# A fused attention and LoRA expert kernel: the last exponential first, router and masks behind the value products, masks read from PSUM, row and gate work of the next batch moved forward

## What is computed

```python
h = _layernorm(x) * (1 + ca) + sa
x = x + ga * attn(h)          # attn: norm, q k v, causal softmax(q k / 16) v, o_proj, + h
h = _layernorm(x) * (1 + cb) + sb
# feed-forward of h:
base_out = silu(gate_base) * up_base @ Wd.T
probs = softmax(xf @ Wr.T); topw, topi = top_k(probs, 2)
# for each chosen expert e, with weight w_e:
hh = silu(gate_base + g_lora_e) * (up_base + u_lora_e)
acc += w_e * (hh @ Ad_e.T @ Bd_e.T * 2)
x = x + gb * (base_out + acc)
```

## Time and profile before

| What | Value |
|---|---|
| Median of three runs | 725.66 us (725.01 to 726.97) |
| Profiled execution, its own time | 727.61 us |
| Its span, first to last instruction | 725.8 us |
| PE busy | 668.1 us, 92% |
| DVE, ACT, POOL busy | 67%, 49%, 55% |
| Page's means: act_s L705, ring_hi L713 on ACT | 598 ns, 627 ns |
| Page's means: ring_lo L453, xT_lo L445, a 128x256 addition (xr L460) on POOL | 1331, 1288, 737 ns |

### The profile page before, as it was taken

One profiled execution on the slowest core, in us unless ns is written; L12 is line 12 of the kernel. 1 busy time (PEld: TensorE's weight loads), 2 busy tenths in 40 slices (PEclk: granted clock), 3 DMA queues, 4 the chain that ended last, 5 costly groups with the idle time before them and its releaser, 6 DMA issues.

```text
span 725.8 us, 10724 instructions
## 1 busy us (share of the span) xinstructions
PE 668.1 (92%) x3760; PEld 568.5 (78%) x3760; DVE 484.9 (67%) x1115; ACT 357.4 (49%) x640; POOL 400.5 (55%) x562
## 2 busy tenths in 40 slices
PE   5679999999969999999969999999997999999995
PEld 3469877978859887878859987887876988788884
DVE  5997685478866775568885767657886668437423
ACT  4634556635534536455435455654553454654542
POOL 3774257538766226547775416753775623743644
PEclk9979999999989999999999999999999999999998
DMA  8200010000000010000000001000000000000000
GB/s 317 92 1 1 1 59 1 1 1 30 0 1 30 1 59 0 1 1 31 1 0 30 1 1 58 1 1 1 30 1 1 30 1 0 1 2 1 30 0 30
DMA packets 14038, 15.45 MB, mean 21 GB/s; under 512 B 1312, under 2 KB 12704, under 8 KB 13984
## 3 DMA queue, kind: packets, MB, share of 16 engines
q1 hardware_dynamic: 13984, 14.76, 6.1%
HBM read 10.57 MB, written 4.19 MB: 20 GB/s over the span
## 4 chain that ended last, share of the span: by engine, by line
PE 64%; DVE 20%; issue 6%; POOL 5%; ACT 2%; DMA 1%; DVEq 0%; POOLq 0%; SPq 0%; ACTq 0%
PE ps L1240 60%; PE ps L1249 5%; DVE tm_hi L1088 3%; POOL ring_lo L453 2%; DVE xr L850 2%; DVE hid L1098 2%; DVE zb L841 1%; DVE tm_lo L1088 1%; DVE zb L838 1%; DMA xs<-in_L_attn_x 1%; DVE gated L859 1%; DVE onehot L1049 1%; DVE tr_full L872 1%; DVE wmask L1105 1%; DVE hid L1096 1%
## 5 line engine op out<-in xcount | busy, mean ns | idle before, releaser
L453 POOL TENSOR_TENSOR ring_lo<-hid,ring_hi 128x512 fp32r<-128x512 f32 x144 | 190.1, 1331 | 107.4 <-ACT ring_hi L713 106.8
L1098 DVE TENSOR_TENSOR hid<-act_s,ps 128x512 f32<-128x512 f32 x120 | 82.4, 686 | 99.6 <-ACT act_s L705 82.6
L705 ACT ACTIVATE act_s<-ps 128x512 f32<-128x512 f32 x120 | 71.7, 598 | 142.6 <-PE ps L1240 142.5
L713 ACT ACTIVATE ring_hi<-hid 128x512 fp32r<-128x512 f32 (+1 forms) x144 | 90.3, 627 | 15.6 <-DVE hid L1096 10.5
L1240 PE MATMUL ps<-wdT_hi,ring_hi 128*128 128x256 f32 x192 | 55.8, 294 | 0.0
L1240 PE MATMUL ps<-wdT_lo,ring_hi 128*128 128x256 f32 x192 | 55.2, 291 | 0.0
L445 POOL TENSOR_TENSOR xT_lo<-tr_full,xT_hi 128x512 fp32r<-128x512 f32 x28 | 35.4, 1288 | 26.4 <-ACT xT_hi L583 26.4
L509 POOL TENSOR_TENSOR tm_lo<-xT_lo,wmask 128x512 fp32r<-128x512 f32 x12 | 18.8, 1591 | 48.1 <-PE ps L1240 48.1
L1240 PE MATMUL ps<-wdT_hi,ring_lo 128*128 128x256 f32 x160 | 45.2, 282 | 0.0
L460 POOL TENSOR_TENSOR xr<-xr,y_gb 128x256 f32<-128x256 f32 x32 | 22.7, 737 | 40.0 <-DVE y_gb L1120 40.0
L1240 PE MATMUL ps<-vv_hi,pT_hi 128*128 128x256 f32 x144 | 43.6, 302 | 0.0
(11 more groups left out here) (223 smaller groups left out, 2131.1 us busy)
## 6 DMA issues: line engine op xcount, KB each, us to landing
xs<-in_L_attn_x SPq DMA_DIRECT2D x4, 1024.0 KB, 5.6
out<-xr SPq DMA_DIRECT2D x7, 512.0 KB, 2.9
s_mod<-in_L_wmod SPq DMA_DIRECT2D x1, 1024.0 KB, 8.6
s_qkvT<-in_L_attn_qkv SPq DMA_DIRECT2D x1, 768.0 KB, 10.1
s_wg<-in_L_ffn_Wg SPq DMA_DIRECT2D x1, 704.0 KB, 7.4
s_wu<-in_L_ffn_Wu SPq DMA_DIRECT2D x1, 704.0 KB, 8.6
s_wd<-in_L_ffn_Wd SPq DMA_DIRECT2D x1, 640.0 KB, 7.6
s_mod<-in_L_wmod SPq DMA_DIRECT2D x1, 512.0 KB, 6.7
```

The source lines that it names most:

```text
L453: pool.tensor_sub(ring[1][:, place(n), :], hid[:, n % HID, :], ring[0][:, place(n), :].bitcast(fp32)).then_inc(h_lo.sem, 1)
L705: nc.scalar.activation(act_s[:, n % 2, :], ps[:, 2 * (n % 2), :], ACT.Silu).then_inc(silu_ready.sem, 1)
L713: nc.scalar.activation(ring[0][p0:P, place(n), :], hid[p0:P, n % HID, :], ACT.Copy).then_inc(h_hi.sem, 1)
L1098: V.tensor_mul(hid[:, n % HID, :], act_s[:, n % 2, :], ps[:, 2 * (n % 2) + 1, :]).then_inc(h_ready.sem, 1)
```

## The change

It changes the order of work on all four engines and the source of one operand; the arithmetic stays.

- `scores_exp` of the last tile goes ahead of the two `tr_high`.
- On PE, `logits(0)` and the masks of the first half go behind the value products, the second mask behind the first half of a base block, in banks 6 and 7 instead of 3 and 2. On DVE `x1_product(6)` goes ahead of `router_shift(0)`.
- `masked(0, m)` reads the mask from PSUM. It still waits for the copy.
- LN2_B: the three Newton steps go from unit 2 to units 6, 7 and 8, the `zb` rows from units 6 and 7 to 8 and 9, the transposes behind one more adapter block.
- Gates go from units 12, 16, 17 to 8 and 9; statistics, rows and z tiles of the next batch to the units in the diff; Newton of LN1_HB from unit 16 to 14.

```diff
-        MASK_BANKS = ((3, 2, 4, 5), (3, 4, 5, 6))
+        MASK_BANKS = ((6, 7, 4, 5), (3, 4, 5, 6))
...
# POOL
-                            if r == 2:
-                                for it in range(NEWTON):
-                                    newton(b, LN2_B, TC, TC, it)
-                            if r == 9:
+                            if r in (6, 7, 8):
+                                newton(b, LN2_B, TC, TC, r - 6)
+                            if r == 10:
...
-                            if r == 16:
+                            if r == 14:
                                 for it in range(NEWTON):
                                     newton(b, LN1_HB, TC, TC, it)
...
# ACT
+                    scores_exp(i)
                     if i == NT - 1:
                         for k in range(KT):
                             tr_high(b, KT * NC + k, xT[0][:, 0, k, :])
-                    scores_exp(i)
...
-                        if ci == 0 and r in (6, 7):
-                            if r == 6:
+                        if ci == 0 and r in (8, 9):
+                            if r == 8:
                                 act.wait_ge(rstd_ready.sem, rstd_ready.at(b, LN2_B))
...
# DVE
                     else:
                         dve.wait_ge(masks_copied.sem, masks_copied.at(b, which))
-                        mask = wmask[:, which, :]
+                    mask = ps[:, MASK_BANKS[ci][which], :]
...
+                x1_product(NT - 2)
                 router_shift(0)
-                x1_product(NT - 2)
...
-                        if r in (7, 8, 10, 11):
+                        if r in (6, 7, 11, 12):
...
-                        if r == 12:
+                        if r == 8:
                             dve.wait_ge(out_ready.sem, out_ready.at(b, -1))
                             gate(b + 1, 0)
-                        if r == 16:
                             gate(b + 1, 1)
+                        if r == 9:
                             gate(b + 1, 2)
-                        if r == 17:
                             gate(b + 1, 3)
...
-                        for i in {4: (0,), 5: (1,), 6: (2,), 7: (3,), 10: (4, 5), 12: (6, 7)}.get(r, ()):
+                        for i in {4: (0,), 5: (1,), 6: (2,), 7: (3,), 8: (4,), 9: (5,), 11: (6, 7)}.get(r, ()):
                             ln1_centre(b + 1, i)
-                        for i in {5: (0,), 6: (1,), 7: (2,), 8: (3,), 11: (4, 5), 13: (6, 7)}.get(r, ()):
+                        for i in {5: (0,), 6: (1,), 7: (2,), 8: (3,), 10: (4, 5), 12: (6, 7)}.get(r, ()):
                             ln1_rows(b + 1, i)
-                        for i in {8: (0, 1, 2), 9: (3,), 12: (4, 5), 14: (6, 7)}.get(r, ()):
+                        for i in {7: (0,), 8: (1, 2), 9: (3,), 12: (4, 5), 13: (6, 7)}.get(r, ()):
                             ln1_stats(i)
...
-                        if r == 15:
+                        if r == 13:
                             moments(range(TC, NT))
...
-                        for i in {13: (0,), 14: (1,), 16: (2, 3)}.get(r, ()):
+                        if r == 16:
+                            dve.wait_ge(rstd_ready.sem, rstd_ready.at(b, LN1_HB))
+                            dve.wait_ge(stored, b * (16 * NC) + 32)
+                        for i in {14: (0, 1), 15: (2, 3), 16: (4, 5), 17: (6, 7)}.get(r, ()):
                             normalise(i, zb, z_ready, z_tile(i))
...
# PE
-                                if ci == 0 and g == 1 and slot == 2 and a == 0:
+                                if ci == 0 and g == 1 and slot == 2 and a == 1:
...
-                probs_values(NT - 2, range(PV_FIRST))
                 logits(0)
-                probs_values(NT - 2, range(PV_FIRST, NT - 1))
                 pe.wait_ge(pt_lo.sem, pt_lo.at(b, NPT - 1))
                 adapter_inputs(0)
-                probs_values(NT - 1, range(PV_FIRST))
+                probs_values(NT - 1)
+                pe.wait_ge(x1_ready.sem, x1_ready.at(b, NT - 2))
+                pe.wait_ge(masks_spread.sem, masks_spread.at(b, 0))
+                mask(0, 0)
+                base(0, 0, 0, (0,))
+                pe.wait_ge(x1_ready.sem, x1_ready.at(b, NT - 1))
+                mask(0, 1)
+                base(0, 0, 0, (1,))
                 pe.wait_ge(shifted_ready.sem, shifted_ready.at(b, 0))
-                pe.wait_ge(masks_spread.sem, masks_spread.at(b, 0))
-                for m in range(2):
-                    mask(0, m)
-                probs_values(NT - 1, range(PV_FIRST, NT))
-                base(0, 0, 0)
-                pe.wait_ge(masks_copied.sem, masks_copied.at(b, 1))
                 base(0, 0, 1)
```

More of the change, by code:

```diff
@@ L748, in body @@
                             nc.scalar.activation(wmask[:, slot, :], ps[:, MASK_BANKS[ci][2 + slot], :], ACT.Copy).then_inc(wmask_ready.sem, 1)
-                        if ci == 0 and r in (6, 7):
-                            if r == 6:
+                        if ci == 0 and r in (8, 9):
+                            if r == 8:
                                 act.wait_ge(rstd_ready.sem, rstd_ready.at(b, LN2_B))
-                            for tile in range(TC + 2 * (r - 6), TC + 2 * (r - 5)):
+                            for tile in range(TC + 2 * (r - 8), TC + 2 * (r - 7)):
                                 normalise(tile, zb[:, tile, :], xr[:, tile, :], z2_ready)
-                        if ci == 0 and r == 9:
+                        if ci == 0 and r == 10:
                             for k in range(KT):
@@ L1078, in masked @@
                         dve.wait_ge(masks_ready.sem, masks_ready.at(b, ci * 4 + which))
-                        mask = ps[:, MASK_BANKS[ci][which], :]
                     else:
                         dve.wait_ge(masks_copied.sem, masks_copied.at(b, which))
-                        mask = wmask[:, which, :]
+                    mask = ps[:, MASK_BANKS[ci][which], :]
                     dve.wait_ge(t_lo.sem, t_lo.at(b, ci * 2 + g))
@@ L1208, in body @@
                             guess(0, TC).then_inc(norm_ready.sem, 1)
-                        if r == 15:
+                        if r == 13:
                             moments(range(TC, NT))
                             guess(TC, TC).then_inc(norm_ready.sem, 1)
-                        if r == 13:
+                        if r == 14:
                             dve.wait_ge(rstd_ready.sem, rstd_ready.at(b, LN1_HA))
-                        for i in {13: (0,), 14: (1,), 16: (2, 3)}.get(r, ()):
+                        if r == 16:
+                            dve.wait_ge(rstd_ready.sem, rstd_ready.at(b, LN1_HB))
+                            dve.wait_ge(stored, b * (16 * NC) + 32)
+                        for i in {14: (0, 1), 15: (2, 3), 16: (4, 5), 17: (6, 7)}.get(r, ()):
                             normalise(i, zb, z_ready, z_tile(i))
-                if not last:
-                    dve.wait_ge(rstd_ready.sem, rstd_ready.at(b, LN1_HB))
-                    dve.wait_ge(stored, b * (16 * NC) + 32)
-                    for i in range(TC, NT):
-                        normalise(i, zb, z_ready, z_tile(i))
                 if not last:
@@ L1380, in body @@
                             transposes(b, KT * NC + k, k, k, [zb[:, tile, :] for tile in range(TC)])
-                    if 2 <= i < NT:
+                    if i >= 2:
                         probs_values(i - 2)
@@ L1493, in units @@
                             for a in range(2):
-                                if ci == 0 and g == 1 and slot == 2 and a == 0:
+                                if ci == 0 and g == 1 and slot == 2 and a == 1:
                                     for k in range(KT):
                                         pe.wait_ge(z2_ready.sem, z2_ready.at(b, NT - 1))
-                                        pe.wait_ge(x1_ready.sem, x1_ready.at(b, NT - 1))
+                                        pe.wait_ge(tm_ready.sem, tm_ready.at(b, 3))
                                         transposes(b, KT * NC + KT + k, 6 + k, k, [zb[:, tile, :] for tile in range(TC, NT)])
```

7 lines of the change are left out of this document (3 added, 4 removed).

## The result

The changed kernel takes 720.18 us (median of four runs, 719.54 to 720.68), the kernel before 725.47 in runs taken beside it (725.01 to 726.97). The ratio is 0.9923, with a 95% interval of 0.9906 to 0.994: 0.8% or 5.3 us faster. The forecast was 713.4, 12.3 us less than before; the time lies inside the range of 705 to 721, but less than half of the gain came.

A forecast was written before the change was run, and what follows sets the result against it. TensorE, busy 92% of the span, bounds the kernel, so only its waits and lower clock can be won. Terms -8.4, +5.6, +16.3 and -1.2 give 12.3 us won: 715.3 on the profiled time, 713.4 on the median, range 705 to 721.

The forecast's parts named there:

- The exponential: Last row's exponential ahead of two xT_hi copies on ACT: PE goes on at 253.1 instead of 254.06, 0.96 us won.
- Masks from PSUM: DVE's five mask products in a batch: 0.68 us each from PSUM, against a median of 1561 ns from SBUF.
- rival 2: Masks from PSUM bring DVE nothing, the five products cost 1.5 us each still: 719.4 us, chance 0.10.
- The change of batch: Query products start at 209.1 instead of 215.09: 6.0 us won at the first two changes, 16.3 in all three.
- rival 3: POOL's early Newton at batch end stands ahead of its input and delays everything behind: 729.7 us, slower, chance 0.10.
- rivals 1 and 4: 1: clock stays up behind the zb wait, 707.4 us, chance 0.20; 4: that wait does not come, 692.2, chance 0.05.
- PE waits 12.1 - 8.35 = 3.8 us: Before the second norm's zb transposes, PE waits 3.8 us for ACT, for POOL, in each batch; bounds 2.5 to 4.5.
- I take 1.5: Price per batch of PE's half clock behind the zb wait: 1.5 us, possible 0 to 3.4.
- small overlaps: Allowance in POOL's chain from the second base block of group 1 to the first zb pair, given as 9.0 us.
- The front of the batch: Up to the second base block of group 1, each batch wins 3.2 us.
- 0.4 taken (0 to 1.4): Second half, behind units 8 and 9: extra DVE work may make hid of unit 10 late, 0.4 us lost, three times.
- The start of the second half: Gates moved behind units 8 and 9: PE's three waits go, 1.9 us won in each of the first three batches.

The follow-up runs named there:

- experiment 8: Experiment 1's kernel with the last row tile's exponential back behind the two xT_hi copies: 700.21 us, ratio 0.9642.
- Experiment 9: The changed kernel (Newton steps at units 6, 7, 8) with the gates back at units 12, 16 and 17: 728.45 us, ratio 1.0032.
- experiment 3: The changed kernel with 32 identity transposes that compute nothing on PE during the wait for zb: 712.59 us, ratio 0.9802.
- experiment 4: The kernel before with only the end-of-batch part: next batch's statistics, rows and z tiles, Newton of LN1_HB at unit 14: 714.7 us, ratio 0.9837.
- experiment 6: Experiment 1's kernel with the gates back at units 12, 16 and 17: 703.46 us, ratio 0.9685.
- experiment 1: The changed kernel with the three LN2_B Newton steps on POOL at units 4, 5, 6 instead of 6, 7, 8: 696.34 us, ratio 0.9581.
- experiment 2: The kernel before with only the second norm's part: Newton steps at units 6, 7, 8, zb rows and transposes later: 753.39 us, ratio 1.0361.

## Why the prediction was right and where it was wrong

**What held.** The direction, and the mechanism of every step. The exponential: 0.96 forecast, 0.97 by experiment 8. Masks from PSUM: 0.68 us for the five products, as taken; rival 2 is refuted, although its time of 719.4 is nearly that measured. The change of batch: 6.0 for the first two forecast, 6.0 and 5.6 measured, 5.0 for the third (4.3 forecast), with waits of 1.07 and 1.07 (1.2 and 1.3 forecast) and no stretch at 0.50; rival 3 did not come. The new wait for zb, released by ACT behind POOL, was there in all four batches with the clock behind it; rivals 1 and 4 did not come.

**The step that failed: "PE waits 12.1 - 8.35 = 3.8 us", with "I take 1.5" for the clock behind it.** Of the 12.3 us that were forecast 5.3 came, so 7.0 are missing: 4.2 in the sum on the profiles, nearly all of them in this step, and 2.8 in the step from the profile to the median (below). Wait and clock were foreseen in kind; their size was not. Together 5.3 were put down for a batch, and the table has 6.3 on the mean (25.0 / 4): 7.1 in the first batch, where a stretch of 6.8 followed, 6.3, 6.0 and 5.7 in the others. The wait itself had an idle time of 4.55, 4.55, 4.31 and 3.93. That is the term that takes 3.8 of the 4.2 us by which the sum of the profiles was off, 2.6 of them by the wait and the rest by the clock; the other terms of the sum missed by up to 2.1 each and nearly cancel. In the first two batches the wait passes even the upper bound of 4.5 that was put on it. Counted as the prediction did, from the second base block at 276.45, the first pair of zb starts 9.83 later, not 9.0, and PE goes on at 12.95, not 12.1. The trace of the changed kernel shows the larger of two causes on POOL's timeline:

```profile
280.71 1.30 POOL L452 TENSOR_TENSOR ring_lo<-hid,ring_hi 128x512 fp32r<-128x512 f32 x1 [0.56 <-ACT ring_hi L711]
281.96 0.20 POOL L412 TENSOR_TENSOR nr_a<-rstd 128x4 f32<-128x4 f32 x1
282.24 0.48 POOL L413 TENSOR_TENSOR nr_a<-nr_a,nr_h 128x4 f32<-128x4 f32 x1
282.80 0.52 POOL L414 TENSOR_TENSOR nr_a<-nr_a,three_halves 128x4 f32<-128x4 f32 x1
...
283.69 1.29 POOL L452 TENSOR_TENSOR ring_lo<-hid,ring_hi 128x512 fp32r<-128x512 f32 x1
...
286.04 0.20 POOL L420 TENSOR_TENSOR shift<-neg_mean,rstd 128x4 f32<-128x4 f32 x1
```

and DVE's at the same time:

```profile
282.25 0.42 DVE L856 TENSOR_SCALAR y_gb<-bc 128x512 f32<-128x512 f32 x1
282.58 0.69 DVE L857 SCALAR_TENSOR_TENSOR gated<-bc 128x512 f32<-128x512 f32 x1
```

The middle third takes 283.60 - 281.96 = 1.64 us, not the 1.1 taken: two of its operations last 0.48 and 0.52 instead of 0.20 while DVE runs the gates, which the same change had put there. The prediction placed the gates where DVE waits for ACT, and asked only what they delay on DVE's own list, not what they do to POOL beside them. Experiment 9 took them away: the same third takes 1.03 there (282.73 to 283.76), and the wait shrank from 4.55 to 3.93, which is also its length in the last batch of the changed kernel, where there are no gates. This 0.6 is shown. With it gone, 3.93 idle or 4.1 with the overlap remains, 0.3 over the estimate. The terms of the prediction's chain add up to 9.3 and it took 9.0, for "small overlaps"; POOL's rows above overlap by 0.04 twice and leave as much between others, so these 0.3 were not there. ACT then does what was foreseen: silu and ring_hi between the two pairs.

```profile
286.28 1.09 ACT L611 ACTIVATE zb<-xr,shift,rstd 128x256 f32<-128x256 f32 x2 [4.35 <-POOL shift L420]
...
288.27 1.08 ACT L611 ACTIVATE zb<-xr,shift,rstd 128x256 f32<-128x256 f32 x2
```

The clock was taken at 1.5, "near the 3.5 us stretch", and measured at 1.9 a batch (experiment 3): in the traces 1.6 behind a stretch of 3.4 and 2.4 in the first batch, behind one of 6.8.

That 720.2 lies inside the range is no merit of the sum. The range reached up to 721 for rival 2, which did not come, and for the bounds of wait and clock.

**Smaller terms.** The front of the batch: 3.2 forecast, 2.8 in batches two to four, 3.8 in the first. The 1.0 more in the first is clock: the stretch at 0.50 at its start lasts to 46.4 in the profile of before and to 44 in that of after. Of the 0.4 missing in the others 0.3 belongs to the change of batch, for in experiment 4, whose front is that of before, this stage takes 68.48 instead of 68.16. "0.4 taken (0 to 1.4)" for hid of unit 10: 1.11 with the overlap, three times, inside its bounds. The reason was named, DVE's operations in SBUF beside POOL, and the value was not; the list of DVE behind unit 9 of the second half has it:

```profile
349.84 1.53 DVE L839 SCALAR_TENSOR_TENSOR zb<-xs,mv,bc 128x256 f32<-128x256 f32 x1
...
352.26 0.89 DVE L807 TENSOR_SCALAR nr_v<-mv 128x4 f32<-128x4 f32 x1
...
353.54 0.69 DVE L1095 TENSOR_TENSOR hid<-act_s,ps 128x512 f32<-128x512 f32 x1
```

The start of the second half gave 2.4 instead of 1.9 (experiment 6 has 2.4 too); the three waits with their overlaps give 1.9. Of the other 0.5 the two traces place 0.4: behind the first two waits the next row starts 0.34 us after the first, where rows start 0.23 apart otherwise, and behind the third the mask's transposes take 0.60 us to the next product instead of 0.36.

**The step from the profile to the median.** The forecast took the gain off the profiled 727.61 and then subtracted 1.9, as if every run of before lost what that one lost. It held two stretches of 6.8 at 0.50, but the runs of before in these comparisons have mean granted clocks from 0.974 to 0.985 and are up to 2.8 us shorter; those of after have 0.978 to 0.982. A part of what was won at the changes of batch is clock that a run of before need not have lost. How much of the 2.8 us this is can't be said, since only one run of before has a trace.

**What the parts are worth.** With the wait for zb out of the way, undoing parts costs 3.9 (exponential), 7.4 (masks' source) and 7.1 (gates); the end of the batch brings 12.1 alone. These add up to 30.5, which is the 30.5 by which experiment 1 beats before. By the ratios it is 31.7, and parts can share a gain, so the match is in part chance. Moving router and masks behind the value products, and taking the Newton steps out of one piece, were not undone by themselves; by this sum little is left for them, but no run shows it.

## What to carry to other kernels

When a chain of small operations is spread over an in-order queue, count from the last piece: what stands ahead of it, and who asks for its result when. Two places sooner on POOL's list turned a gain of 0.8% into one of 4.2%. A wait can cost more than its length: those of 3.9 to 4.6 us cost 1.9 more each on average through PE's clock, two of 1.07 nothing. So short waits can be better than their sum in one, and work moved into a gap of one engine must be priced by what it slows on the engine beside it.

## What the runs showed of the hardware that was not expected

- Where DVE and POOL both work in SBUF, the instruction that starts second can last until the other has ended, however small it is. On DVE, a 128x4 operation takes 0.16 to 0.17 us alone. nr_v, started at 352.26 during a ring_lo, takes 0.89 and ends 0.03 behind it; in experiment 2 one takes 1.26 and ends 0.02 behind the ring_lo that had started just before it, and hid behind it is late by as much:

```profile
282.44 0.16 DVE L812 TENSOR_SCALAR nr_i<-nr_v 128x4 int32<-128x4 int32 x1
282.63 1.26 DVE L813 TENSOR_SCALAR rstd<-nr_i 128x4 int32<-128x4 int32 x1
283.81 1.27 DVE L1097 TENSOR_TENSOR hid<-act_s,ps 128x512 f32<-128x512 f32 x2
```

- It goes the other way too: POOL's 128x4 operations go from 0.20 to 0.48 and 0.52 beside DVE's gates, and end 0.06 behind y_gb and gated. The Trainium skill, "GPSIMD Engine Reference", section "8. Key points", has GpSimd contend with DVE instructions that run in a 2-port mode or have two SBUF inputs; gated, which reads its tile twice, agrees. y_gb reads one input, and whether it runs in such a mode no run here shows.
- Not every DVE instruction is held up: in the changed kernel hid, which reads act_s and PSUM, takes its usual 0.69 at 281.44 beside a ring_lo.
- Transposes of fp32 by the identity, 3.65 us of them in a wait of 4.7, kept PE's clock at 1.00 (experiment 3).
- The length of the stretch at 0.50 behind one and the same idle time is not fixed: 3.93 us idle was followed by 3.4 us in the last batch of the changed kernel, by 6.8 us in experiment 2, and by either in experiment 9.
